# Attention and mixture-of-experts kernel: a third shared-expert unit ahead of the expert loop, and a new order of the matmuls around the token lists

## The reference

```
flat = layernorm(x).reshape(n, d)                  # n = 1024 tokens, d = 256
logits = flat @ Wr.T + 0.5 * dom                   # dom: a small network on the mean of each batch
topk_idx = top_k(logits + router_bias, 4)          # 64 experts, 4 for each token
combine = scores of the four, normalised to sum 1
g, u = flat @ Wg[e], flat @ Wu[e]                  # every expert: 256 -> 64
out = sum over e of (silu(g) * u * combine[:, e]) @ Wd[e]
for i in range(2):                                 # two shared experts, for all tokens
    sh = silu(flat @ Sg[i]) * (flat @ Su[i])       # 256 -> 256
    out = out + sh @ Sd[i]                         # 256 -> 256
return x + out
```

## Time and profile before

| | us |
|---|---|
| median of 3 runs | 218.74 (216.85 to 219.05) |
| the profiled execution, its time | 218.63 |
| its span in the trace | 216.9 |
| TensorE busy in the span | 175.2 (81%) |
| VectorE busy | 133.2 (61%) |
| GpSimd busy | 111.2 (51%) |
| ScalarE busy | 88.7 (41%) |

### The profile page before, as it was taken

One profiled execution on the slowest core, in us unless ns is written; L12 is line 12 of the kernel. 1 busy time (PEld: TensorE's weight loads), 2 busy tenths in 40 slices (PEclk: granted clock), 3 DMA queues, 4 the chain that ended last, 5 costly groups with the idle time before them and its releaser, 6 DMA issues.

```text
span 216.9 us, 4118 instructions
## 1 busy us (share of the span) xinstructions
PE 175.2 (81%) x964; PEld 124.1 (57%) x965; DVE 133.2 (61%) x528; ACT 88.7 (41%) x270; POOL 111.2 (51%) x121
## 2 busy tenths in 40 slices
PE   0980259999789999999999979999998979978300
PEld 0460148654435787777777968888863457437200
DVE  2995982175896574899997755556640450485450
ACT  2637378315522565565555654555552110120000
POOL 6692211001067454576666674676402777677740
PEclk9999999999855899999999999999999999999975
DMA  6899999995022333355454342544321333244432
GB/s 137 269 385 349 348 359 366 384 363 177 0 59 78 110 91 116 107 151 154 142 145 118 112 129 76 145 132 126 113 86 65 110 92 104 85 122 144 126 119 69
DMA packets 29825, 34.50 MB, mean 159 GB/s; under 512 B 4248, under 2 KB 27561, under 8 KB 29680
## 3 DMA queue, kind: packets, MB, share of 16 engines
q1 hardware_dynamic: 25392, 25.90, 36.1%
q0 software_dynamic: 4416, 8.41, 15.0%
HBM read 27.99 MB, written 9.96 MB: 175 GB/s over the span
## 4 chain that ended last, share of the span: by engine, by line
PE 68%; DVE 14%; ACT 4%; issue 4%; POOL 4%; DMA 3%; POOLq 1%; DVEq 0%; ACTq 0%
PE pb L1083 13%; PE pb L923 12%; PE pb L1047 9%; PE pb L1014 7%; PE pb L1051 6%; PE pb L1070 4%; PE pb L1119 3%; POOL z L394 3%; PE pb L984 2%; PE pb L1072 2%; DVE sc L558 2%; DMA proj_sb<-in_proj 2%; PE pb L888 2%; PE pb L894 2%; PE pb L908 2%
## 5 line engine op out<-in xcount | busy, mean ns | idle before, releaser
L362 POOL DMA_INDIRECT xg<-z_rows,tok x32 | 32.9, 1029 | 29.1 <-issue 11.6
L394 POOL DMA_INDIRECT z<-y_slots,slot_i x32 | 32.5, 1017 | 21.4 <-DMA y_slots<-ysb 11.3
L1083 PE MATMUL pb<-wd_sb,hT 128*128 128x256 f32 (+1 forms) x120 | 37.6, 396 | 0.0
L374 POOL DMA_INDIRECT xg<-z_rows,tok_now x28 | 27.9, 998 | 14.4 <-issue 11.5
L923 PE MATMUL pb<-zT,shared_sb 128*128 128x512 f32 x64 | 33.5, 675 | 0.7 <-ACT ysb L513 0.7
L805 DVE COPY xgT<-pb 128x256 f32<-128x256 f32 x60 | 25.3, 423 | 11.6 <-PE pb L1014 10.6
L513 ACT ACTIVATE ysb<-pb 128x256 f32<-128x256 f32 x60 | 23.0, 383 | 12.2 <-PE pb L1083 11.4
L1014 PEld LDWEIGHTS pb<-ident,xg 128*128 128x128 f32 x120 | 22.7, 198 | 8.4 <-issue 5.3
L1014 PE MATMUL pb<-ident,xg 128*128 128x128 f32 x120 | 25.5, 296 | 2.0 <-issue 1.4
L494 ACT ACTIVATE sg<-pb 128x64 f32<-128x64 f32 x60 | 13.4, 223 | 30.1 <-PE pb L1047 19.1
L1047 PE MATMUL pb<-wgu_sb,xgT 128*64 128x128 f32 x256 | 22.4, 299 | 0.3 <-DVE xgT L805 0.3
(11 more groups left out here) (166 smaller groups left out, 242.9 us busy)
## 6 DMA issues: line engine op xcount, KB each, us to landing
wgu_sb<-in_wgu SPq DMA_DIRECT2D x8, 1024.0 KB, 10.4
y_slots<-ysb SPq DMA_DIRECT2D x60, 128.0 KB
wd_sb<-in_wd SPq DMA_DIRECT2D x4, 1024.0 KB, 11.6
shared_sb<-in_shared SPq DMA_DIRECT2D x1, 1536.0 KB, 9.3
xs<-in_x SPq DMA_DIRECT2D x4, 256.0 KB, 4.1
z_rows<-z SPq DMA_DIRECT2D x4, 256.0 KB, 9.1
out<-xs SPq DMA_DIRECT2D x8, 128.0 KB, 1.9
xg<-z_rows,tok POOLq DMA_INDIRECT x32, 2.9
```

The costliest lines, as they stand in the source:

```text
L362: g.indirect_dma_start(xg[:, n, :], None, z_dram, bass.IndirectOffsetOnAxis(ap=tok[:, t:t + 1], axis=0), bounds_check=N - 1, oob_is_err=Fa ...
L374: g.indirect_dma_start(xg[:, n, :], None, z_dram, bass.IndirectOffsetOnAxis(ap=tok_now[:, n:n + 1], axis=0), bounds_check=N - 1, oob_is_er ...
L394: g.indirect_dma_start(z[:, j % NC, :].bitcast(I32), None, y_dram, bass.IndirectOffsetOnAxis(ap=slot_i[:, 0, j:j + 1].bitcast(U32), axis=0 ...
L1083: t.matmul(pb[4 + n][:, 0:D], hT[:, n, :], wd_sb[:, q, :] if pair else wd_sb[:, bass.ds(d_of[k], 1), :].rearrange("p o d -> p (o d)"), sta ...
```

## The change

The third unit (number 2) moves from behind the loop to ahead of it, into banks 4 and 5 (`EARLY` = 3, and a table of banks). The four matmuls of unit 1, two of which stood ahead of the four list rounds and two behind L992, now stand one behind each round. On VectorE `turn_numbers` stands ahead of `slots`, since unit 2's second bank was in use by the values that it reads; unit 2's product stands in step 1 of the loop.

```diff
--- before.py
+++ after.py
@@ -53,7 +53,8 @@
 GU_LAG, D_LAG = 1, 3
 LG_BANK = (4, 6)
 NC = 8
-EARLY = 2
+EARLY = 3
+UNIT_BANKS = ((0, 1), (2, 3), (4, 5), (2, 3), (0, 1), (2, 3), (0, 1), (2, 3))
 NR = NJ // GJ
 
 
@@ -460,10 +461,9 @@
                 act.wait_ge(unit_ps, n + 1)
                 if n >= 2:
                     act.wait_ge(unit_h, n - 1)
-                bank = 2 * (n % 2)
-                a.activation(sgu_v[:, 0, n % 2, :], pb[bank][:, :], ACT.Silu).then_inc(unit_sb, 1)
+                a.activation(sgu_v[:, 0, n % 2, :], pb[UNIT_BANKS[n][0]][:, :], ACT.Silu).then_inc(unit_sb, 1)
                 if n < EARLY:
-                    a.activation(sgu_v[:, 1, n % 2, :], pb[bank + 1][:, :], ACT.Identity).then_inc(unit_sb, 1)
+                    a.activation(sgu_v[:, 1, n % 2, :], pb[UNIT_BANKS[n][1]][:, :], ACT.Identity).then_inc(unit_sb, 1)
 
             def value(r, tiles, base):
 
@@ -757,8 +757,8 @@
                 one_hot(r, NP, pair_lanes, 0, 0)
             needs()
             tokens(tok[:, :], pb[6][:, 128:128 + NP], NP, NR, 1)
+            turn_numbers()
             slots()
-            turn_numbers()
 
             def pick_choice(j):
 
@@ -785,15 +785,17 @@
 
                 i, hc, blk = units[n]
                 dve.wait_ge(unit_sb, 2 * n + 2 if n < EARLY else EARLY + n + 1)
-                u = sgu_v[:, 1, n % 2, :] if n < EARLY else pb[2 * (n % 2) + 1][:, :]
+                u = sgu_v[:, 1, n % 2, :] if n < EARLY else pb[UNIT_BANKS[n][1]][:, :]
                 v.tensor_tensor(hsh[:, 2 * i + hc, blk * 512:(blk + 1) * 512], sgu_v[:, 0, n % 2, :], u,
                                 ALU.mult).then_inc(unit_h, 1)
 
-            for n in range(EARLY):
+            for n in range(EARLY - 1):
                 unit(n)
 
             def step(which, k, first, s):
 
+                if s == 1:
+                    unit(EARLY - 1)
                 tile = which(0)
                 if tile:
                     pair, q, m, r = tile
@@ -920,7 +922,7 @@
                 elif n >= EARLY + 2:
                     pe.wait_ge(unit_h, n - 1)
                 for h in halves:
-                    ins = t.matmul(pb[2 * (n % 2) + g][:, :], sgu_sb[:, i, g, h, hc * P:(hc + 1) * P],
+                    ins = t.matmul(pb[UNIT_BANKS[n][g]][:, :], sgu_sb[:, i, g, h, hc * P:(hc + 1) * P],
                                    zT[:, h, blk * 512:(blk + 1) * 512], start=(h == 0), stop=(h == DC - 1),
                                    skip_group_check=True)
                 if g and 1 in halves:
@@ -975,7 +977,6 @@
                 ins = t.matmul(pb[5][0:E, 0:P], chosen[:, i, :], ones_bf[:, :], start=(i == 0), stop=(i == NT - 1))
             ins.then_inc(count_ps, 1)
             unit(0, 1, (1,))
-            unit(1, 0)
 
             def list_tokens(r, tiles, base, col):
                 pe.wait_ge(onehot, 2 * (base + r + 1))
@@ -987,6 +988,7 @@
 
             for r in range(NR):
                 list_tokens(r, NP, 0, 128)
+                unit(1, r // 2, (r % 2,))
             pe.wait_ge(need_ok, 2)
             pe.wait_ge(code_ok, 1)
             t.matmul(pb[7][:, :].rearrange("p (i e) -> p i e", e=E), need_bf[:, :],
@@ -995,7 +997,10 @@
             t.matmul(pb[5][0:E, 256:257], tri[0:E, 0:E], need_bf[:, 0:1], start=True, stop=True, skip_group_check=True)
             t.matmul(pb[5][0:1, 260:261], need_bf[:, 0:1], ones_bf[0:E, 0:1], start=True, stop=True,
                      skip_group_check=True).then_inc(base_ps, 1)
-            unit(1, 1)
+            pe.wait_ge(logit_sb, 2)
+            unit(2, 0)
+            pe.wait_ge(turns_step, 1)
+            unit(2, 1)
 
 
             pe.wait_ge(unit_sb, 2)
@@ -1035,7 +1040,7 @@
                     at = q if pair else q + NP
                     pe.wait_ge(xT_sb, at + 1)
                     if pair and q == 0:
-                        pe.wait_ge(unit_sb, 2 * EARLY)
+                        pe.wait_ge(unit_sb, 4)
                     if not pair or q >= 2:
                         pe.wait_ge(h_ok, at - 1)
                     if pair:
@@ -1075,6 +1080,8 @@
                     pair, q, m, r = tile
                     n = m % 2
                     at = q if pair else q + NP
+                    if pair and q == 0:
+                        pe.wait_ge(unit_sb, 2 * EARLY)
                     pe.wait_ge(hT_sb, at + 1)
                     if not pair or q >= 2:
                         pe.wait_ge(y_sb, at - 1)
```

## The result

| | before | after |
|---|---|---|
| median, same chip | 217.80 (4 runs, 216.06 to 219.05) | 222.27 (4 runs, 221.01 to 222.91) |
| ratio, 95% interval | | 1.0204 [1.0106, 1.0301] |
| the profiled execution | 218.63 | 222.91 |
| its span | 216.9 | 221.2 |

The account below looks back on a forecast made before the run. VectorE's run behind the base offsets was taken to set the loop's start, GpSimd's gathers the end. 218.63 + 1.1 (front) + 1.8 (tail) = 221.5 us; range 219.0 to 226.0, the forecast's own 220.4 to 222.6.

Parts of the forecast that it names:

- The two terms of the sum: Front: fifth tile's matmul 1.1 us later, at 75.6; tail: gathers and everything behind them 1.8 us later.
- Base offsets: Ahead of the loop: L992 at 61.69 instead of 58.93, +2.76 us; first expert matmul at 68.65.
- I take it that it holds: Ahead of the loop: the granted clock stays up through the list rounds, judged by the tail's bursts, not by much.
- the first hole: Ahead of the list rounds: TensorE empty from 53.1 to 55.6, with only one matmul of unit 0 left there.
- The first rival: Clock falls in the new hole at 53 to 56 us; fifth tile at 79 to 81, 225.4 us; chance 0.34.
- the -1.9: First loop steps: if the clock stays up, four steps and a list round take 7.0 us instead of 8.9.
- The tail term: Behind the loop: 13th gather held +2.5 us, the old hold of 0.7 at the 17th gone, net +1.8 us.
- The place of the 13th gather: In the tail: goes out at 184.8 instead of 182.32, waiting for choice 4, which stands behind unit 5.
- the 17th: In the tail: this gather, due at 190.0, no longer waits for VectorE; its old hold of 0.7 us goes.
- +1.1 us for the whole loop behind it, which has one step rate in both kernels: Loop: the fifth tile's delay, 75.6 instead of 74.55, carries through unchanged.
- The second rival: Tail: the end hangs on TensorE's units, not the gathers, so 3.43 us go; 216.3 us; chance 0.08.
- the third: Tail: 13th gather not held, old hold of 0.7 goes, front costs 1.1; 219.0 us; chance 0.10.

Follow-up runs that it names:

- experiment 1: The changed kernel run again with no edit, on another chip: 235.45 us against 230.5 for the kernel before, ratio 1.0181.
- experiment 2: The kernel before with only unit 1's four matmuls placed one behind each list round: 234.28 us, ratio 1.0125.
- experiment 4: The changed kernel with slots ahead of turn numbers again: one run, 235.05 us (kernel before: 231.59).
- experiment 8: Twenty register moves on TensorE ahead of the loop, added to experiment 5: 237.47 us, ratio 1.0185.
- experiment 5: The changed kernel with VectorE's tail order one group later, unit 5 behind choices 4 to 7: 235.85 us, ratio 1.0168.
- experiment 9: Eight one-column matmuls on TensorE ahead of the loop, added to experiment 5: 238.28 us (4 runs, too scattered for a ratio).
- experiment 6: The kernel before with VectorE's tail order one group earlier, three units ahead of the first choices: one run, 235.81 us (before: 231.59).
- experiment 3: The changed kernel with unit 1's matmuls as before, two ahead of the rounds and two behind the base offsets: 232.93 us, ratio 1.0072.
- experiment 11: The kernel before with VectorE's tail order one group of four choices later from unit 5 on: 232.37 us against 234.45, ratio 0.9904.
- experiment 10: The kernel before with eight one-column matmuls added on TensorE ahead of the loop: 235.21 us against 234.45, ratio 1.0042.
- experiment 7: The kernel before with one unit ahead of the loop instead of two, VectorE's tail order fitted to that: 235.02 us, ratio 1.0135.

## Why the prediction was right, and where it was not

**The verdict and its two places held.** Slower, from both ends of the loop, at 222.27 against 221.5: inside the range, and inside the forecast's own 220.4 to 222.6. The two terms of the sum, +1.1 and +1.8, measured +1.02 and +1.93. The profiled execution, for which the sum was made, took 222.91 instead of 221.5: that is the loop's 1.35, which the sum put at nothing.

**Base offsets.** Forecast 61.69, measured 61.35. Right, and the front is bound by VectorE's run behind them: 68.00 - 61.35 = 6.65 us, forecast 6.96.

**The clock.** The step "I take it that it holds" came out in the first trace of the changed kernel for the first hole only. The second hole, 66 to 68, was not seen: the unit no longer fills TensorE's wait once it is done at 65.5. Four steps took 7.57 us instead of 7.0. The two misses, -0.65 and +0.57, cancel, and the fifth tile stood at 75.57 against the forecast 75.6: that this term came out to 0.1 us is luck. What the clock gave back was 8.86 - 7.57 = 1.3 us, not 1.9.

**The first rival's fall happens, and its price was too high.** Of seven traces with alternating rounds the clock fell behind the first hole in four (experiments 1, 2, 4 and 8) and not in three (after, 5 and 9). With the whole change the fifth tile then stood at +23.30, +22.04 and +22.01 behind round 0, against +19.93, +20.57 and +19.98: 2.3 us on average, not the 3.4 to 5.4 between 75.6 and 79 to 81. The clock came back while the pieces were still running, and the rival had it low until the loop. The Trainium skill ("TensorE: Matmul & The Clock Gate", "HAM oscillation") has idle gaps between bursts of matmuls send the clock down. Four of the traces agree; in the other three the same gap of 2.20 us left the clock at 1.00. That the hole is the cause is not shown either. With the old order, and an idle time of about 0.5 us ahead of round 0, the clock fell in all five traces, in three of them at the same time, some 2 us into the rounds (experiment 6 here; experiments 3 and 11 are like it):

```profile
56.00:58.00 2.00, 1.47 (x21) 1.29 (x21) 1.72 (x5) 1.31 (x4) 0.00 (x0) 0.74 0.00 0
...
62.00:64.00 2.00, 1.40 (x3) 0.32 (x2) 1.83 (x11) 1.09 (x2) 1.39 (x3) 0.56 0.26 82
64.00:66.00 2.00, 1.50 (x12) 1.04 (x12) 1.32 (x5) 0.22 (x1) 1.70 (x2) 1.00 0.17 47
```

**What was there to be given back.** The trace of before had the clock low until 72. In experiments 6 and 11, which have the same front, it was back at 64, and the fifth tile stood at +17.07 and +17.09 instead of +18.89. There the -1.9 was never to be had. The forecast named this, but the sum took the one trace at its word. On the same chips the fifth tile of the changed front stood at +22.01 (experiment 8) and +19.98 (experiment 9): 4.9 and 2.9 us later, where the first pair had 1.04. Up to the unit start 4.4 and 0.6 us of that were left. So what the front costs at the fifth tile went from 1.0 to 4.9 us over three pairs of traces, and the forecast's 1.1 fits one of them.

**The tail term** was off by 0.1: +1.93 against +1.8. The place of the 13th gather came to 0.01 us, and the 17th was free. The mechanism is shown by moving VectorE's order alone, one way (experiment 6) and the other (5 and 11). The late rows, which the forecast lacked, cost nothing in the changed kernel, because the first gather could come at +4.94 and the 13th be due 12 x 1.30 = 15.6 us later, at +20.5, still ahead of 21.14.

**What failed** is "+1.1 us for the whole loop behind it, which has one step rate in both kernels". The loop gave 1.35 us more. It is the wait of 1.42 for a gathered tile that ends at 130.03; the changed kernel on another chip shows one standstill there, not two (experiment 1), so it isn't a fixed price of the change. The trace holds a hint: the gather of that tile went out at 125.15, and between 126.75 and 127.00 an instruction packet falls among its rows (q0). Before, the same tile's gather went out at 124.12 and had its rows through when the packet came, behind 127.75.

```profile
q8 instruction: 1, 0.02, 38.6%
q0 software_dynamic: 4, 0.02, 32.2%
```

So it may be the same meeting as in the tail. No run tests it, and the cause stays open.

**The second rival**, that the tail gives a unit's 3.43 us back, fell with the 13th gather; the third, in which the 13th is not held, with the same.

## What to carry to other kernels

Work moved off a busy engine is worth what the queue behind it gives back: here GpSimd's gathers set the end, and shifting a unit of TensorE's work only shifted VectorE's written order against eight buffers. When an order is written out by hand, recount it against the buffers for each change of what stands ahead of it. And look at a granted clock in several executions before counting on getting it back.

## What the runs showed of the hardware

**An instruction packet can hold data up.** One packet of 0.02 MB among the last rows of `y_slots` delayed their landing: in eight traces in which it came 0.7 to 1.5 us behind the unit start, the first gather was at +4.2 to +4.9; in five in which it came 6.1 us or more behind, at +2.7 to +2.8. Sixteen more instructions on TensorE before the loop moved it from one case to the other (experiment 10), though not in experiment 9. The Trainium skill ("Runtime: NRT & Kernel Launch", "Instruction fetch mechanics") has an engine's sequencer refill its buffer in 16 KiB blocks over a DMA queue of its own, and the fetch mostly hidden. The packet's size agrees. Hidden it was for TensorE, which ran its units behind the unit start without a wait (163.65 and 166.02 on), but not for the transfer beside it.

**Chips differ by more than the change.** The kernel before took 217.80 us on the first chip and 230.5 to 234.5 on three others, with the granted clock at 1.00 in the loop there too (experiment 1, 80 to 180 us). There ScalarE showed waits that end "<-remote", up to 2.3 us each in the loop, and in the tail it took units 4 to 10 us after TensorE was through with them (the row of experiment 7 and experiments 5, 8 and 9), and TensorE waited for VectorE and ScalarE in steps that it never waited in on the first chip. Neither trace of the first chip has such a wait. What they are stays open.
